# Second cross attention: two turns side by side on TensorE, and the copies in a matching order

## The reference, cut to what matters

```python
kv_input = jnp.concatenate([layernorm(ctx), latn], axis=1)      # 1601 + 64 keys, 128 wide
q, (k, v) = latn @ Wq, jnp.split(kv_input @ Wkv, 2, axis=-1)    # 16 heads of 64
weight = softmax(einsum('bhld,bhnd->bhln', q * scale, k * scale))
out = einsum('bhln,bhnd->bhld', weight, v) ... @ Wo
x = x + out
```

## Time and profile before

| | |
|---|---|
| median of 3 runs | 1957.34 us (1953.15 to 1957.87) |
| the profiled execution's own time | 1956.76 us |
| its span | 1955.0 us |
| PE busy | 1723.9 us, 88% of the span |
| DVE, ACT, POOL busy | 1235.9, 856.8, 520.6 us |

### The profile page before, as it was taken

One profiled execution on the slowest core, in us unless ns is written; L12 is line 12 of the kernel. 1 busy time (PEld: TensorE's weight loads), 2 busy tenths in 40 slices (PEclk: granted clock), 3 DMA queues, 4 the chain that ended last, 5 costly groups with the idle time before them and its releaser, 6 DMA issues. The chain is left out here.

```text
span 1955.0 us, 33370 instructions
## 1 busy us (share of the span) xinstructions
PE 1723.9 (88%) x11692; PEld 1213.1 (62%) x11692; DVE 1235.9 (63%) x3060; ACT 856.8 (44%) x1939; POOL 520.6 (27%) x707
## 2 busy tenths in 40 slices
PE   5799999999997996389999999999999999999423
PEld 2466666666666885366766766667666666665322
DVE  6466666666664773766666666666666656654477
ACT  2255555555652443244444444444444444433222
POOL 1000000000002221235432354333542345400223
PEclk9599999999998998699999999999999999999665
DMA  4535353535220012200000000000000000000000
GB/s 110 140 86 119 85 119 85 119 85 119 68 52 1 22 66 101 72 18 29 29 12 28 17 28 28 11 17 28 28 18 21 17 28 28 1 1 1 0 6 5
DMA packets 32659, 90.35 MB, mean 46 GB/s; under 512 B 8552, under 2 KB 17424, under 8 KB 32528
## 3 DMA queue, kind: packets, MB, share of 16 engines
q1 hardware_dynamic: 32528, 88.71, 16.9%
HBM read 40.43 MB, written 8.91 MB: 25 GB/s over the span
## 5 line engine op out<-in xcount | busy, mean ns | idle before, releaser
L2075 PE MATMUL c_pv_ps<-c_prob_t,c_xn 128*128 128x512 f32 (+2 forms) x896 | 413.3, 598 | 0.0
L340 ACT ACTIVATE c_prob<-c_score_ps,c_neg_max 128x512 f32<-128x512 f32 (+1 forms) x512 | 304.4, 607 | 64.8 <-PE c_scratch L2061 35.0
L873 DVE TENSOR_REDUCE a_chunk_max<-a_side_ps 128x1 f32<-128x512 f32 (+1 forms) x416 | 260.9, 665 | 109.7 <-PE a_side_ps L694 109.5
L359 DVE TENSOR_REDUCE c_chunk_max<-c_score_ps 128x1 f32<-128x512 f32 (+1 forms) x512 | 291.2, 582 | 46.7 <-PE c_score_ps L266 45.2
L237 PE MATMUL c_turn_ps<-consts,c_prob 128*128 128x128 f32 (+2 forms) x1792 | 285.4, 276 | 11.6 <-DVE c_prob_t L369 10.9
L237 PEld LDWEIGHTS c_turn_ps<-consts,c_prob 128*128 128x128 f32 (+2 forms) x1792 | 212.0, 139 | 96.5 <-issue 32.2
L2075 PEld LDWEIGHTS c_pv_ps<-c_prob_t,c_xn 128*128 128x128 f32 (+2 forms) x896 | 158.4, 191 | 164.6 <-issue 164.5
L373 DVE COPY c_prob_t<-c_turn_ps 65x128 f32<-65x128 f32 (+1 forms) x256 | 61.6, 280 | 298.2 <-PE c_turn_ps L237 298.2
L806 ACT ACTIVATE a_prob<-a_st_ps 128x1024 f32<-128x1024 f32 (+1 forms) x224 | 214.5, 959 | 66.9 <-PE a_st_ps L678 66.9
L266 PE MATMUL c_score_ps<-c_x_hi,c_q_hi 128*128 128x512 f32 (+1 forms) x512 | 218.2, 426 | 2.4 <-ACT c_prob L340 1.6
L324 ACT ACTIVATE c_prob_t<-c_turn_ps 128x512 f32<-128x512 f32 x128 | 76.4, 597 | 274.0 <-PE c_turn_ps L237 272.7
(11 more groups left out here) (287 smaller groups left out, 2607.4 us busy)
## 6 DMA issues: line engine op xcount, KB each, us to landing
a_stack<-a_k_hi SPq DMA_DIRECT2D x128, 200.1 KB, 4.1
a_stack<-a_k_lo SPq DMA_DIRECT2D x64, 200.1 KB, 4.2
a_ctx<-in_ctx_dram SPq DMA_DIRECT2D x16, 768.0 KB
c_ctx<-in_ctx_dram SPq DMA_DIRECT2D x16, 768.0 KB
absorbed_queries<-b_q_out SPq DMA_DIRECT2D x16, 512.0 KB, 3.4
c_q_raw<-absorbed_queries SPq DMA_DIRECT2D x16, 512.0 KB, 3.3
w<-in_L_ffn_w_dram SPq DMA_DIRECT2D x2, 512.0 KB
fold_raw<-in_L_xattn_Wkv_dram SPq DMA_DIRECT2D x2, 512.0 KB
```

Of the source, the lines that this page charges most:

```text
L340: nc.scalar.activation(prob[s % 2][:, cols], score_ps[:, cols], ACT.Exp, bias=neg_max[:, s % 2:s % 2 + 1], accum_out=sums[:, (s // QUAD) % ...
L359: nc.vector.reduce_max(chunk_max[:, s % 2, c:c + 1], score_ps[:, quad_chunk(c, keys)], AX_X).then_inc(chunk_max_done, 1)
L873: nc.vector.reduce_max(out, rows, AX_X).then_inc(side_taken, 1)
L2075: last = nc.tensor.matmul(lay.own.pv_ps[:], t.xn[m][0:rows, i, :], lay.own.prob_t[u][0:rows, i, :], start=(i == 0), stop=(i == LAT))
```

## The change

PE does two chunks of scores, then both turns that follow, and the same again: S0 S1 T0 T1 S2 (b) S3 V (a) T2 T3. ACT copies T2 behind its four exponentials instead of ahead of them. DVE takes the four maxima without anything between, then `c_neg_max`, then the copies of T0 and T1, the b job, the three statistics; the copy of T3 stands at the start of the next slot, ahead of its maxima and behind the a job. The number of matmuls, transposes, copies and bytes is the same, and so are the semaphores on which each step waits.

```diff
@@ PE, in the loop over chunks and behind V
-                    if before and c != 2:
-                        turn(k, kind, s, min(c, 2))
+                    if before and c == 1:
+                        turn(k, kind, s, 0)
+                        turn(k, kind, s, 1)
...
                 if before:
-                    turn(k, kind, s, CHUNKS - 1)
+                    turn(k, kind, s, 2)
+                    turn(k, kind, s, 3)
@@ ACT
                 at(k, kind, s, "b")
-                if not (kind == "first" and s == 0):
-                    copy_turned(k, kind, s)
...
                     if c == 1:
                         at(k, kind, s, "a")
+                if not (kind == "first" and s == 0):
+                    copy_turned(k, kind, s)
@@ DVE
-                maximum(k, s, 0)
-                lay.dve_between(dve, k, kind, s, 0)
                 if s and (s - 1, "a") in table[kind]:
                     lay.dve_take(dve, table[kind][s - 1, "a"], base(kind, k), k, kind, s - 1)
-                if before:
-                    copy_turned(k, kind, s, 0)
-                for c in range(1, CHUNKS):
+                if s >= 2 or kind != "first":
+                    copy_turned(k, kind, s - 1, 3)
+                for c in range(CHUNKS):
                     maximum(k, s, c)
-                    if c < CHUNKS - 1:
-                        lay.dve_between(dve, k, kind, s, c)
...
                                         negate=True).then_inc(neg_max_done, 1)
+                if before:
+                    copy_turned(k, kind, s, 0)
+                    copy_turned(k, kind, s, 1)
                 if (s, "b") in table[kind]:
                     lay.dve_take(dve, table[kind][s, "b"], base(kind, k), k, kind, s)
-                if before:
-                    copy_turned(k, kind, s, 1)
-                    copy_turned(k, kind, s, 3)
+                for c in range(CHUNKS - 1):
+                    lay.dve_between(dve, k, kind, s, c)
...
         body(BODIES - 1, "last")
+        copy_turned(BODIES, "mid", -1, 3)
```

## The result

| | before | after |
|---|---|---|
| median | 1956.36 us (1953.15 to 1957.87, 6 runs) | 1965.23 us (1961.9 to 1967.4, 6 runs) |
| profiled execution, its span | 1956.76, 1955.0 us | 1967.4, 1965.6 us |

The ratio is 1.0042, 95% interval 1.0028 to 1.0056: 8.9 us slower, a small but real loss. The forecast was 1964.5.

The account below looks back on a forecast made before the run. PE was taken as the bound, busy 932.7 of 940 us, its work unchanged. Waits added, 19.0 us, less 11.1 taken away made 7.9 slower: 1956.8+7.9 = 1964.7, stated as 1964.5, range 1954 to 1970.

Parts of the forecast that it names:

- What the change takes away: PE's waits on DVE at the loop's branch (7.4 us), in slots 1 and 9 (2.7), smaller ones (1.0): together 11.1 us.
- Slots 1 and 9: T2 starts 0.30 us after S3's last matmul instead of 0.11; this 0.19, fourteen times, goes: 2.7 us.
- Turns side by side cost nothing: On PE, a turn costs 0.44 us behind a turn as behind scores; 0 taken for the regrouping.
- Norm slots: Slots 3, 7, 11, 15: T0 waits for ACT's copy of T2, 0.35 us each, 30 times: 10.5 us added.
- Slots 4 and 12: Slots with context transposes: T0 waits 0.3 us for ACT's copy of T2, 15 times: 4.5 us added.
- Slots 0 and 8: Short V, and DVE's copy of T3, which T1 needs, comes late: 0.1 us, 15 times, 1.5 us added.
- The output slot: ACT's exponentials and copy of T2 take about 1.86 of the 2.04 us available: price 0, cover only 0.2.
- After the last body: T0 waits for the copy of T2; values start 4.6 us after the first turn, 1.8 us more.
- T2 behind POOL's wait: Slot 4 of the first body: T2 was under PE's 3.64 us wait, now stands behind it: 0.7 us added.
- The first body: Slots ahead of slot 4 may be late by 0.2 us each at no cost, hidden by the wait for POOL's tile.
- The roof of 11.1: The 11.1 us of PE waits taken away was also called the most the change could gain.
- The clock rival: Some 60 short PE waits lower the granted clock oftener, 10 to 20 us more: 1975 to 1985; chance 0.05.

Follow-up runs that it names:

- DVE's move alone: The kernel before, with only DVE's copy of T3 moved to the start of the next slot, ahead of maximum 0: 1941.19 us, ratio 0.9931.

## Why the prediction was right, and where its steps were off

**What the change takes away** held, and was a little more. The branch is under the values, and the 1.49 us at each return is gone. Slot 0 behind a return took 7.6 us from scores to scores and 5.99 without one, since V was 0.1 late too: 1.6 each, 8.1 instead of 7.4. Slots 1 and 9 gave back 0.2 fourteen times (2.8), slots 3 and 11 0.08 each (1.0), together 11.9. DVE's move alone shows it without the rest, and putting it back costs again.

**Turns side by side cost nothing**, as predicted: S0 S1 T0 T1 take 0.77 + 0.69 + 0.79 = 2.25 us, twice 1.13 before. But the other half of the regrouping was not free. Without T2 between them, S3 to the values, the values and both turns take 0.28 + 3.48 + 0.57 = 4.33, before 0.28 + 0.46 + 3.43 + 0.14 = 4.31. 0.02 in some 120 slots is 2.4 us that the sum did not have.

**Norm slots.** Predicted 0.35, with T0 2.35 to 2.4 us behind T2; measured 2.36 and 0.37. Of this 0.31 is the wait and 0.06 the start of the scores behind T1 (0.85 us after T0 instead of 0.79). 30 times: 11.1 for 10.5. **Slots 4 and 12**: predicted 0.3, measured 0.37; 5.2 in fourteen slots for 4.5. **Slots 0 and 8**: 1.5 predicted, 0.1 in each, for a late copy of T3. Only slot 1 of the loop's six bodies shows it, T1 being 0.13 late; slot 9 and the last body show 0.02 at most: 0.8 in all. T2 takes 0.06 more there to the next scores, but so did T3 before (0.19 for 0.14). From `c_u_t` to that copy it is 1.32 us on DVE, as in the earlier trace rows. **The output slot** cost nothing, as said. **After the last body** 2.0 instead of 1.8. **T2 behind POOL's wait** in slot 4 of the first body: from the context transposes to the next scores 2.01 us instead of 1.16, 0.85 for the 0.7 predicted.

**The first body: the step that failed.** "The slots ahead of it may be late by 0.2 each at no cost, for the same wait hides them" is wrong. That wait is on POOL, and POOL's start hangs on DVE's statistic of slot 2, in the same queue as the copies: it moves with the slots instead of hiding them. Here the error cost little: most of the 1.9 us by which the head is longer is the clock in slot 1. Its size shows in DVE's move alone: the statistic comes 6.2 us after its slot's S0 instead of 7.5, since it no longer stands behind the copy of T3, and the context transposes come 1.3 earlier. That is half of the 2.4 us the sum had no place for. The other 1.2 lie behind those transposes, in the same work, and are the clock again: it stood at 1.2 GHz for 6.8 us around them before and after the change, and for 3.4 with DVE's move alone.

**The roof of 11.1 was none.** It counted the waits behind the head (11.9 as measured) and left out the head and the clock's dip. DVE's move gained 14.8.

**The clock rival did not happen.** The 44 waits of 0.37 left the granted clock at 1.00 over the whole stretch. The opposite came: the dip of before, about 1.3 us, vanished together with the long waits at the return, and came back once where waits of 0.5 to 0.8 us were put there. That is two dips at ten returns in two profiles. With ACT's move undone, PE waits 1.14 us in every slot, and the clock fell to 1.2 GHz for 3.4 us five times behind the first body (at 951.6, 1463.6, 1610.3, 1757.1 and 1903.9), each time within 0.2 us of the end of such a wait. The six profiles in which PE has no wait over 0.3 us there have no dip. That such waits cause the dips is therefore likely; but most of them brought none, what picks the one is open, and no run tests it by itself.

The two profiles add up as follows. From the first values to the turns after the last body +6.8, of which the parts explain 6.3: 11.1 + 5.2 + 0.8 + 2.4 = 19.5 added, less 11.9 and the dip's 1.3. Then +2.0 from those turns to the values, +1.9 in the head, +1.5 behind and -1.6 ahead of the stretch, both in code that is the same. That makes the 10.6 us between the profiled executions; between the medians it is 8.9. The sum was made against the profiled execution and gave 7.9. So that the forecast came within 1 us of the median is partly luck: 2.4 for S3 to the values and 1.3 for the two kinds of wait were missing, against 0.7 too much for slots 0 and 8, 0.8 too little taken away and 1.3 for the dip, and the head's clock fell in this profile and not in two of the seven with the turns side by side.

## What to carry to other kernels

When producer and consumer are moved to new places in hand-written queues, look at what stands between the consumer and its earliest moment: here two exponentials ahead of one copy cost 0.37 us in six of sixteen slots, and moving that copy ahead of them on ACT mends it. Take a change apart before judging it: a loss of 8.9 us held a gain of 14.8 in one of its moves. A step that "a wait hides anyway" is only hidden if the engine waited for does not itself hang on that step; follow its chain back first.

## What the runs showed of the hardware

- At the loop's branch VectorE began nothing for 2.5 to 2.7 us in every return of two profiles (2.48 to 2.56 before, 2.50 to 2.74 with the copy of T3 put back), and PE lost nothing of its own: after the change slot 0 behind a return takes 6.38 us and slot 8 with the same work 6.39. It was free under the values, where DVE is idle for 2.72 us at a return and 2.73 in slot 8 without one.
- Eight transposes in a row, in each slot of the changed kernel, took 0.79 us to the next scores (0.85 behind a wait), and from 850 to 1790 us the granted clock stayed at 1.00; only in slots 1 and 5 of the first body, where it was at 1.2 GHz, they took more (1.56 in slot 1). The Trainium skill ("TensorE: Matmul & The Clock Gate", Part 4: PE-mode transpose) says that transposes do not count as PE-busy in the same way as other matmuls; amid scores and values, no run here shows harm from it.
- The clock fell at the end of single long waits (2.48 and 3.33 us in slot 2 of the first body) and behind none of the 44 of 0.37. A wait of 1.64 us ahead of slot 1 left it at 2.4 GHz before, one of 1.70 was followed by 1.2 GHz after. The length did not decide it, for with ACT's move undone one of 1.64 was followed by 1.2 GHz too; what differed was whether the clock had risen ahead of the wait.
